# A graph network layer pair on one core: when each piece of the weights is asked for, and the queue that brings x

## The chip, the cores and the metric

The kernel runs on 1 core of one Trainium2 chip. The metric is the device time of one execution in microseconds. Six things work side by side in a core: TensorE (PE for its matmuls, PEld for the loading of its stationary operand), VectorE (DVE), ScalarE (ACT), GpSimd (POOL), SyncE (SP, here only an issuer of transfers) and 16 DMA engines.

## The reference

There are 96 nodes with 1024 features, 1632 edges, float32 throughout.

```python
h = relu(layernorm(x))
q, k, v = h @ wq.T + bq, h @ wk.T + bk, h @ wv.T + bv
q2, k2, v2 = q @ wiq.T + biq, k @ wik.T + bik, v @ wiv.T + biv      # 16 heads of 64
mask = -inf [N, N]; mask[src, dst] = softplus(type_weights)[edge_type - 1]
attn = softmax(q2 @ k2.T / 8 + mask)
x = x + (attn @ v2) @ wo.T + bo

h = relu(layernorm(x))
u = h @ root + bias
for r in range(8):                     # mean of the neighbours over edges of type r
    u = u + mean_r(h[src]) @ weight[r]
z = concat([u, h]) @ w_gate + b_gate
x = x + tanh(u) * z + h * (1 - z)
```

That makes 18 matrices of 1024x1024 (seven of the first layer, root, eight relations, and w_gate as two), 4 MB each and each used once: some 75 MB are read from HBM for an activation of only 96 rows.

## The kernel before, in words

The 18 matrices are read in the order of `SEQUENCE` (wq, wk, wiq, wik, wv, wiv, wo, root, the half of w_gate for x, the eight relations, the half of w_gate for u). Each is cut into four pieces of 1 MB (`PIECES`), so there are 72 pieces, numbered n = 0 to 71. A piece is 128 partitions x 2048 float32: half of the input features (four chunks of 128) by half of the output columns.

The pieces go through a ring of six slots of 1 MB in SBUF (`raw`, `SLOTS`). SyncE does nothing but ask for them. Its `fetch(n)` waits until piece n - 6 has been used (`piece_used`), because that piece sat in the same slot, and then issues the piece's transfers. The first four pieces go as one transfer of 1 MB each, all others as two of 512 KB (`transfers(n)`), the first with the even partitions, the second with the odd ones, one directly behind the other. `landed(n)` is the semaphore value of the slot that says that all of piece n is there.

TensorE walks through the same 72 pieces in the same order, in `piece` (L779), and in `gate_piece` (L1026) for the last four. A piece is 64 matmuls of a 128x64 block of weights against 96 columns, each with its own load of weights: four column chunks (`c`), four input chunks (`k`), two groups of 64 columns (`g`). The first waits for `landed(n)`; the last raises `piece_used`. Between pieces TensorE does the small work: transposes, the comparing of edges (L809, L820), the scores (L838), attn times v2 (L855), and the sums over neighbours (`sum_messages`, L967, behind the second piece of matrix WG_X, which is between pieces 33 and 34). DVE, ACT and POOL prepare and take what these need.

At the start x comes in two halves of 192 KB, columns 0 to 511 by SyncE's queue (ahead of the weights) and columns 512 to 1023 by ScalarE's queue (ahead of the biases, the edge lists and the type weights). DVE takes the statistics of each half (`bn_stats`, L504), and TensorE transposes x (L790). Then come the centring (L508), the transposing (L871), the copy into `uT` by ACT (L408) and the first piece.

Of the kernel before, what the change touches and what calls it, by code (L numbers as in the profile page):

```python
# [30 lines left out]
SLOTS = 6  # L31
# [5 lines left out]
def kind_of(n):  # L37
    return (KINDS_WIV if SEQUENCE[n // PIECES] == WIV else KINDS)[n % PIECES]


def transfers(n):

    return 1 if n < 4 else 2


def landed(n):

    return 16 * sum(transfers(i) for i in range(n % SLOTS, n + 1, SLOTS))
# [9 lines left out]
def gnn_kernel(nc, x, weights, biases, edge_columns, edge_rows, type_weights, out):  # L58
# [3 lines left out]
    CH = C // 2  # L62
# [17 lines left out]
    with ExitStack() as ctx:  # L80
        def sb(name, shape, dt=F32):
            return ctx.enter_context(nc.sbuf_tensor(name, shape, dt))

        def sem(name):
            return ctx.enter_context(nc.semaphore(name))

        raw = sb("raw", [P, SLOTS, CH * HALF])
        x_sb = sb("x_sb", [N, D])
# [74 lines left out]
        x_landed = [sem(f"x_landed{b}") for b in range(2)]  # L163
# [4 lines left out]
        raw_landed = [sem(f"raw_landed{s}") for s in range(SLOTS)]  # L168
        out_landed = sem("out_landed")
        piece_used = sem("piece_used")  # L170
        consts_ready = sem("consts_ready")
        vec = sem("vec")
        pool = sem("pool")
# [87 lines left out]
        def first_piece(m):  # L261
            return PIECES * SEQUENCE.index(m)
# [8 lines left out]
        def bank(t, b):  # L271
            return t[:, b, 0:TW]

        def half(t, b):
            return t[:, b * TW:(b + 1) * TW]

        def cols(t, b):
            return t[:, b * HALF:(b + 1) * HALF]
# [17 lines left out]
        @block.sync  # L296
        def _(sp):
            def fetch(n):
                where = PIECES * SEQUENCE[n // PIECES] + kind_of(n)
                if n >= SLOTS:  # L300
                    sp.wait_ge(piece_used, n - SLOTS + 1)
                for j in range(transfers(n)):
                    part = slice(j, P, transfers(n))
                    sp.dma_start(raw[part, n % SLOTS, :], weights[where, part]).then_inc(raw_landed[n % SLOTS], 16)

            sp.dma_start(cols(x_sb, 0), cols(x, 0)).then_inc(x_landed[0], 16)
            for n in range(N_PIECES):
                fetch(n)
            sp.wait_ge(out_first, 2)
            sp.dma_start(cols(out, 0), cols(out_rows, 0)).then_inc(out_landed, 16)  # L310
            sp.wait_ge(out_last, 1)
            sp.dma_start(out[:, D - P:D], out_rows[:, D - P:D]).then_inc(out_landed, 16)
            sp.wait_ge(out_landed, 48)
# [80 lines left out]

        @block.scalar
        def _(act):
            act.dma_start(cols(x_sb, 1), cols(x, 1)).then_inc(x_landed[1], 16)
            act.dma_start(bias_rows[:, :], biases.rearrange("m (c p) -> (m c) p", p=P)).then_inc(bias_landed, 16)
            act.dma_start(row_i, edge_rows).then_inc(rows_landed, 16)
            act.dma_start(edge_i[:, :], edge_columns).then_inc(edges_landed, 16)  # L400
# [368 lines left out]
        def _(pe):  # L769
            def piece(n, moving, a, opens=True, closes=True):  # L770

                s, kind = n % SLOTS, kind_of(n)
                b, k0 = kind // 2, CH * (kind % 2)
                pe.wait_ge(raw_landed[s], landed(n))
                for c in range(CH):
                    for k in range(CH):
                        for g in range(2):
                            at = k * HALF + c * P + g * HD
                            mm = pe.matmul(a[g * HD:(g + 1) * HD, b, c * N:(c + 1) * N], raw[:, s, at:at + HD],  # L779
                                           moving(k0 + k), start=opens and k0 == 0 and c == 0 and k == 0,  # L780
                                           stop=closes and k0 > 0 and c == CH - 1 and k == CH - 1)
                mm.then_inc(piece_used, 1)

            def of(t):
# [90 lines left out]
            n = first_piece(WQ)  # L875
            pe.wait_ge(h_ready, 2)
            piece(n, of(rT), acc[0])
            show_keys(0)
            show_keys(1)
            pe.wait_ge(diag_ready, 1)  # L880
            pe.wait_ge(h_ready, 4)
            pe.matmul(acc[1][:, 0, 0:N], ones_f[:, :], scale_diag[:, :], start=True, stop=True).then_inc(scale_shown, 1)
            piece(n + 1, of(rT), acc[0])
            piece(n + 2, of(rT), acc[0])
            piece(n + 3, of(rT), acc[0])

            n = first_piece(WK)
# [7 lines left out]
            n = first_piece(WIQ)  # L895
# [7 lines left out]
            n = first_piece(WIK)  # L903
# [7 lines left out]
            n = first_piece(WV)  # L911
# [8 lines left out]
            n = first_piece(WIV)  # L920
# [10 lines left out]
            n = first_piece(WO)  # L931
# [41 lines left out]
            n = first_piece(ROOT)  # L973
# [9 lines left out]
            for b in range(2):  # L983
                mm = pe.matmul(bank(side, b), ones[0:N, :], half(counts, b), start=True, stop=True)
# [8 lines left out]
            n = first_piece(WG_X)  # L993
# [9 lines left out]
            for r in range(R):  # L1003
                n = first_piece(REL0 + r)
# [29 lines left out]
            n = first_piece(WG_U)  # L1034
# [55 lines left out]
```

## Time and profile before

| | us |
|---|---|
| median of 3 runs | 228.63 (226.9 to 232.76) |
| the profiled execution, own time | 230.86 |
| its span, first to last instruction | 228.7 |
| PE busy | 217.3 (95%) |
| PEld busy | 210.8 (92%) |
| DVE / ACT / POOL busy | 80.5 / 22.3 / 24.6 |

The profiled execution is one execution; its own time is 2.16 us longer than its span. Busy time of PE is the union of its matmuls as recorded. PE and PEld work side by side. The part of the page with 40 slices shows the TensorE clock at nine tenths or more of full speed in each of them.

### The profile page before, as it was taken

What the parts mean: (1) busy time and instruction counts of PE and PEld (TensorE: products, weight loads), DVE (VectorE), ACT (ScalarE), POOL (GpSimd) and SP (SyncE); (2) the same over time, 40 slices, a digit from 0 to 9 for tenths busy, and PEclk for the clock granted to TensorE, in tenths of its full rate; (3) what the DMA queues carried; (4) which work ended last, traced back from release to release, by engine and by line L of the source; (5) the groups of instructions that cost most, each with busy time, mean ns of one, the idle gap of its engine ahead of it and who ended that gap; (6) DMA issues with size and microseconds to landing.
All of it is one profiled execution on the core that took longest, in us unless ns stands there. A gap on an engine that the chain in (4) does not pass through costs nothing.

```text
span 228.7 us, 10049 instructions
## 1 busy us (share of the span) xinstructions
PE 217.3 (95%) x4797; PEld 210.8 (92%) x4797; DVE 80.5 (35%) x138; ACT 22.3 (10%) x41; POOL 24.6 (11%) x53
## 2 busy tenths in 40 slices
PE   1999998999999999999999999999999999999894
PEld 1889998999999999799989999999999888999893
DVE  2459838051499731457466500000000000000614
ACT  2523000000020120313051000000000000000001
POOL 2255005400000000010003910000000000000000
PEclk9999999999999999999999999999999999999999
DMA  6999999999989989948981999999999999999202
GB/s 224 381 392 419 426 420 408 398 398 387 393 307 380 388 312 322 386 146 308 335 341 37 391 401 390 384 387 393 393 403 374 388 378 376 386 397 337 110 3 69
DMA packets 12363, 76.99 MB, mean 337 GB/s; under 512 B 2554, under 2 KB 2818, under 8 KB 3108
## 3 DMA queue, kind: packets, MB, share of 16 engines
q1 hardware_dynamic: 11792, 75.95, 85.9%
q8 instruction: 37, 0.61, 1.0%
q10 hardware_dynamic: 532, 0.42, 0.6%
q14 instruction: 2, 0.02, 0.0%
HBM read 75.97 MB, written 0.39 MB: 334 GB/s over the span
## 4 chain that ended last, share of the span: by engine, by line
PE 94%; DMA 2%; issue 1%; DVE 1%; ACT 0%
PE acc L779 81%; PE acc L1026 4%; DMA x_sb<-in_x 2%; PE turn L967 1%; PE side L827 1%; PE side L967 1%; PE side L1026 1%; PE turn L855 1%; DVE stats L504 1%; PE acc L797 1%; PE turn L797 0%; PE turn L871 0%; PE side L838 0%; PE turn L838 0%; PE acc L871 0%
## 5 line engine op out<-in xcount | busy, mean ns | idle before, releaser
L779 PE MATMUL acc<-mean,raw 128*64 128x96 f32 x2048 | 85.5, 246 | 1.4 <-issue 1.4
L779 PEld LDWEIGHTS acc<-mean,raw 128*64 128x64 f32 x2048 | 84.9, 137 | 1.8 <-issue 1.8
L779 PE MATMUL acc<-hT,raw 128*64 128x96 f32 x1024 | 44.7, 247 | 0.2
L779 PEld LDWEIGHTS acc<-hT,raw 128*64 128x64 f32 x1024 | 42.9, 137 | 1.5 <-issue 1.2
L742 DVE TENSOR_TENSOR uT<-acc,uT 128x384 f32<-128x384 f32 x2 | 1.1, 558 | 83.0 <-PE acc L779 83.0
L779 PE MATMUL acc<-qT,raw 128*64 128x96 f32 x512 | 22.0, 246 | 1.0 <-issue 1.0
L779 PEld LDWEIGHTS acc<-qT,raw 128*64 128x64 f32 x512 | 21.4, 137 | 1.3 <-issue 1.3
L779 PE MATMUL acc<-kT,raw 128*64 128x96 f32 x512 | 21.7, 246 | 0.0
L779 PEld LDWEIGHTS acc<-kT,raw 128*64 128x64 f32 x512 | 21.3, 137 | 0.3 <-issue 0.3
L779 PE MATMUL acc<-uT,raw 128*64 128x96 f32 x256 | 13.0, 271 | 0.0
L779 PEld LDWEIGHTS acc<-uT,raw 128*64 128x64 f32 x256 | 12.6, 156 | 0.3 <-ACT uT L408 0.2
L392 POOL TENSOR_TENSOR mean<-mean,per_count 128x384 f32<-128x384 f32 x8 | 8.4, 1079 | 23.5 <-DVE per_count L700 23.5
L465 ACT ACTIVATE gateT<-uT 128x384 f32<-128x384 f32 x2 | 1.0, 524 | 91.7 <-DVE uT L742 91.7
L1026 PE MATMUL acc<-uT,raw 128*64 128x96 f32 x192 | 8.7, 247 | 0.7 <-issue 0.7
L1026 PEld LDWEIGHTS acc<-uT,raw 128*64 128x64 f32 x192 | 8.3, 137 | 0.9 <-issue 0.9
L337 POOL TENSOR_TENSOR moments<-moments,pow_args 96x1 f32<-96x1 f32 x2 | 1.3, 636 | 56.6 <-DVE moments L683 56.5
L645 DVE STREAM_TRANSPOSE attnT<-attn 32x512 f32<-32x512 f32 x9 | 6.3, 701 | 0.3
L426 ACT ACTIVATE attn<-attn 96x768 f32<-96x768 f32 x2 | 1.7, 845 | 46.4 <-DVE attn L618 46.4
L790 PE MATMUL side<-ident,x_sb 96*128 96x96 f32 x8 | 1.5, 371 | 4.6 <-DMA x_sb<-in_x 4.6
L790 PEld LDWEIGHTS side<-ident,x_sb 96*128 96x128 f32 x8 | 1.2, 223 | 4.6 <-issue 4.6
L700 DVE RECIPROCAL per_count<-per_count 128x192 f32<-128x192 f32 x4 | 5.3, 1335 | 0.0
L580 DVE TENSOR_SCALAR mean<-node_iota,edge_tmp 102x384 f16<-102x384 f16 x16 | 5.3, 400 | 0.0
(177 smaller groups left out, 149.7 us busy)
## 6 DMA issues: line engine op xcount, KB each, us to landing
raw<-in_weights SPq DMA_DIRECT2D x136, 512.0 KB, 5.6
raw<-in_weights SPq DMA_DIRECT2D x4, 1024.0 KB, 9.8
x_sb<-in_x SPq DMA_DIRECT2D x1, 192.0 KB, 3.7
x_sb<-in_x ACTq DMA_DIRECT2D x1, 192.0 KB, 3.8
out<-out_rows SPq DMA_DIRECT2D x1, 192.0 KB, 2.1
out<-out_rows ACTq DMA_DIRECT2D x1, 144.0 KB, 2.2
out<-out_rows SPq DMA_DIRECT2D x1, 48.0 KB, 2.5
bias_rows<-in_biases ACTq DMA_DIRECT2D x1, 36.0 KB
```

The lines of the kernel that those rows point to most:

```text
L392: gp.tensor_tensor(mean[:, c, TW:2 * TW], mean[:, c, TW:2 * TW], half(per_count, 1), ALU.mult).then_inc(mean_later, 1)
L504: dve.bn_stats(stats[:, b, :], cols(x_sb, b)).then_inc(vec, 1)
L580: dve.tensor_scalar(rel_hot[:, c, :], node_iota[:, :], rel_key_f[:, c:c + 1], rel_step_f[:, c:c + 1], ALU.is_equal, ALU.mult).then_inc(rel ...
L645: dve.transpose(squares(attnT, j, i), squares(attn, i, j)).then_inc(attn_turned, 1)
L700: dve.reciprocal(span, span).then_inc(per_count_ready, 1)
L779: mm = pe.matmul(a[g * HD:(g + 1) * HD, b, c * N:(c + 1) * N], raw[:, s, at:at + HD], moving(k0 + k), start=opens and k0 == 0 and c == 0 a ...
L790: t = pe.transpose(dst[:, b, c * N:(c + 1) * N], src[:, (b * CH + c) * P:(b * CH + c + 1) * P], ident[0:N, 0:N])
L797: t = pe.transpose(dst[0:N, b, c * P:(c + 1) * P], src[:, (b * CH + c) * N:(b * CH + c + 1) * N], ident[:, :])
L827: pe.matmul(side[0:N, 0, 0:TW], src_hot[:, c, :], rel_hot[:, c, :], start=c == 0, stop=c == EC - 1).then_inc(counted, 1)
L855: mm = pe.matmul(turn[odd * HD:(odd + 1) * HD, h, j * N:(j + 1) * N], v2[0:N, head * HD:(head + 1) * HD], attnT[:, at:at + N], start=True, ...
L967: mm = pe.matmul(bank((turn, side)[c % 2], b), msgs[s][:, c * P:(c + 1) * P], half(counts, b), start=s == 0, stop=s == 1)
L1026: mm = pe.matmul(z[g * HD:(g + 1) * HD, :], raw[:, s, at:at + HD], of(uT)(k0 + k), start=k0 == 0 and k == 0 and (c == 0 or alone), stop=k0 ...
```

## The change

Three edits.

- **When a piece is asked for.** `lead(n)` is new: 4 for pieces 0 to 31, 5 for 32 to 38, 6 from 39 on. The first transfer of piece n now waits for piece n - lead(n) to be used. Four pieces go out without a wait, where six did.
- **Half a piece for half a piece.** The second transfer no longer follows directly. It waits until half of piece n + 1 - lead(n) has been used. For this `piece` raises a new semaphore, `step_used`, at the last matmul of its second column chunk.
- **x.** Both halves of x go out from SyncE's queue, one behind the other, ahead of the weights. ScalarE's queue now begins with the biases.

```diff
+STEPS = 2
+
 def transfers(n):
-
-    return 1 if n < 4 else 2
+    return 1 if n < lead(n) else STEPS
+
+
+def lead(n):
+    return 4 if n < 32 else 5 if n < 39 else SLOTS
...
             def fetch(n):
                 where = PIECES * SEQUENCE[n // PIECES] + kind_of(n)
-                if n >= SLOTS:
-                    sp.wait_ge(piece_used, n - SLOTS + 1)
                 for j in range(transfers(n)):
+                    if n >= lead(n) and j == 0:
+                        sp.wait_ge(piece_used, n + 1 - lead(n))
+                    if n >= lead(n) and j > 0:
+                        sp.wait_ge(step_used, (STEPS - 1) * (n + 1 - lead(n)) + j)
                     part = slice(j, P, transfers(n))
                     sp.dma_start(raw[part, n % SLOTS, :], weights[where, part]).then_inc(raw_landed[n % SLOTS], 16)
 
-            sp.dma_start(cols(x_sb, 0), cols(x, 0)).then_inc(x_landed[0], 16)
+            for b in range(2):
+                sp.dma_start(cols(x_sb, b), cols(x, b)).then_inc(x_landed[b], 16)
...
         def _(act):
-            act.dma_start(cols(x_sb, 1), cols(x, 1)).then_inc(x_landed[1], 16)
             act.dma_start(bias_rows[:, :], biases.rearrange("m (c p) -> (m c) p", p=P)).then_inc(bias_landed, 16)
...
+                    if c < CH - 1 and (c + 1) * STEPS % CH == 0:
+                        mm.then_inc(step_used, 1)
                 mm.then_inc(piece_used, 1)
```

## Rows read from the trace of the kernel before

**Rows 1.** The page, parts 1 and 2: engines, and the span in 40 slices.
```profile
PE 217.3 (95%) x4797; PEld 210.8 (92%) x4797; DVE 80.5 (35%) x138; ACT 22.3 (10%) x41; POOL 24.6 (11%) x53
DMA  6999999999989989948981999999999999999202
```

**Rows 2.** Waits of PE: who waited for what, us in total, times, longest.
```profile
PE side L790 <- DMA x_sb<-in_x: 4.6, 1, 4.6
PE acc L779 <- issue: 2.3, 4, 1.0
```

**Rows 3.** Waits of SyncE's queue, the same columns.
```profile
SPq L304 <- PE acc L779: 124.5, 66, 7.7
```

**Rows 4.** VectorE's timeline, two takes behind neighbouring pairs of pieces: start, duration.
```profile
53.76 0.56 DVE L489 TENSOR_TENSOR k2T<-acc,bias_cols 128x384 f32<-128x384 f32 x1 [5.04 <-PE acc L779]
56.40 0.56 DVE L489 TENSOR_TENSOR k2T<-acc,bias_cols 128x384 f32<-128x384 f32 x1 [2.08 <-PE acc L779]
```

**Rows 5.** The chain that ended last: start, us, what; all its pauses over 0.04 us after 8 us.
```profile
30.25 0.13 issue
...
36.21 0.96 issue
...
58.45 0.05 issue
...
180.19 0.51 issue
180.70 5.50 PE acc L779 x128
186.20 0.42 issue
186.62 5.50 PE acc L779 x128
192.12 0.42 issue
...
213.97 0.72 issue
```

**Rows 6.** The page, part 3: the queue of instructions; packets, MB, share of 16 engines.
```profile
q8 instruction: 37, 0.61, 1.0%
```

**Rows 7.** Transfers in 34.6 to 34.8, 178.4 to 178.6 and 128.0 to 128.2 us.
```profile
q8 instruction: 1, 0.02, 33.2%
...
q8 instruction: 1, 0.02, 30.0%
...
q8 instruction: 1, 0.02, 29.1%
```

**Rows 8.** Weight transfers (L304) asked for in 16-34, 34-56, 56-100, 150-172, 172-192 us.
```profile
DMA to landing us min/median/max: 6.8/7.9/9.1
...
DMA to landing us min/median/max: 4.6/5.5/8.0
...
DMA to landing us min/median/max: 3.8/4.8/6.6
...
DMA to landing us min/median/max: 4.9/5.6/6.9
...
DMA to landing us min/median/max: 4.6/6.2/8.3
```

**Rows 9.** Weight transfers asked for in 1.2-1.3 (piece 0) and 123.5-123.6 us (half of piece 40).
```profile
DMA to landing us min/median/max: 6.3/6.3/6.3
...
DMA to landing us min/median/max: 3.7/3.7/3.7
```

**Rows 10.** Windows: stretch, length, engines' busy time; last columns: granted clock, DMA share, GB/s.
```profile
38.00:56.00 18.00, 18.00 (x442) 18.00 (x440) 5.02 (x15) 0.00 (x0) 4.56 (x9) 1.00 1.01 398
178.00:196.00 18.00, 16.65 (x393) 16.20 (x391) 0.00 (x0) 0.00 (x0) 0.00 (x0) 1.00 0.99 381
```

**Rows 11.** Timeline of 0 to 16 us, the way to the first piece: start, duration, instruction.
```profile
0.81 0.39 SPq L306 DMA_DIRECT2D x_sb<-in_x  x1
0.81 0.42 ACTq L397 DMA_DIRECT2D x_sb<-in_x  x1
...
4.50 1.28 DVE L504 BATCH_NORM_STATS2 stats<-x_sb 96x6 f32<-96x512 f32 x2 [4.50 <-DMA x_sb<-in_x]
4.61 1.51 PE L790 MATMUL side<-ident,x_sb 96*128 96x96 f32 x8 [4.61 <-DMA x_sb<-in_x]
...
7.93 4.87 PE L779 MATMUL acc<-uT,raw 128*64 128x96 f32 x64
```

More of the change, by code:

```diff
@@ L170, in gnn_kernel @@
         piece_used = sem("piece_used")
+        step_used = sem("step_used")
         consts_ready = sem("consts_ready")
```

## The prediction

> **What bounds the kernel now.** I read the page first. TensorE is busy for 95% of the span, and so are the DMA engines in most slices [rows 1]. Two resources near their limit are a warning: busy shares alone don't say which one the other waits for. The waits do. In PE's list the only wait for a transfer is the one for x at the very start, 4.6 us; no piece of weights is ever waited for [rows 2]. SyncE's queue, in turn, waits 66 times for PE to free a slot, 124.5 us in all [rows 3]. So the transfers run ahead and the matmuls set the pace.
>
> That pace is read from VectorE's takes behind two neighbouring pieces of wik: 56.40 - 53.76 = 2.64 us for a piece of 64 matmuls [rows 4]. Against it 1 MB (1.049 million bytes) in 2.64 us is 397 GB/s, and the DMA engines move 398 at a share of 1.01 where PE runs without a break [rows 10]. There is next to no spare rate. 72 pieces at 2.64 us are 190 of the 228.7 us. The rest is PE's small work, the start, and pauses.
>
> The pauses are the third thing to read, from the chain that ended last [rows 5]. Seven times PE stands still in the middle of a run of matmuls with nothing to wait for that the profile knows ("issue"). Two things give away what they are. The last three before 196 us lie exactly 128 matmuls apart, which with their 128 loads are 256 instructions. And the page has a queue of instructions with 37 packets and 0.61 MB [rows 6], some 16 KB each, while PE and PEld ran 2 x 4797 = 9594 instructions [rows 1], which is 37.5 times 256. So PE's program itself arrives over the DMA engines, 256 instructions at a time, among the weights. Such a packet begins in 178.4 to 178.6 and PE goes on at 180.70; one begins in 34.6 to 34.8 and PE goes on at 36.21 + 0.96 = 37.17 [rows 5, 7]. A block is thus usable 2.1 to 2.6 us after its packet begins. Stepping back from the pause at 180.19 in blocks of 2 x 2.64 = 5.28 us gives 132.67 for an earlier block's first need; its packet began at 128.0 to 128.2 [rows 7], usable by 130.4, with 2.2 us to spare, and there was no pause. The pauses are packets of instructions that came late.
>
> What a pause costs is more than its idle time, since the last matmul's recorded end covers some. From 180.70 to 186.62 are 5.92 us for a block that takes 5.28: 0.64 lost where the chain shows 0.42, so 0.22 is to be added to each. The first three: 0.13 + 0.96 + 0.05 + 3 x 0.22 = 1.80 us. The last four: 0.51 + 0.42 + 0.42 + 0.72 + 4 x 0.22 = 2.95 us. Together 4.75 us.
>
> Why late? The time from asking for weights to their landing says how much data stands in line. A half piece with nothing before it takes 3.7 us [rows 9]. By stretch the median is 7.9 us in 16-34, 5.5 in 34-56, 4.8 in 56-100, 5.6 in 150-172 and 6.2 in 172-192 [rows 8]. Four of the seven pauses follow the two stretches with a line of 6 us and more. The pause at 58 us costs little and 214 us is near the end, so the tie isn't strict, but it is what speaks for the change.
>
> **The change part by part.**
>
> *Lead of four, halves asked for apart (pieces 4 to 31, to about 100 us).* The first half of piece n is asked for when three pieces are still to be used, so it has 3 x 2.64 = 7.92 us. The second half goes 1.32 us later and has 6.6 us. Transfers that are spaced like this need 3.7 us when nothing is in line, or 4.5 if a half follows a half at the rate of 1.32 us (3.7 + 1.32 - 0.52, the spacing of two issues being about 0.5). That leaves 2 us or more, so no wait of PE; the line before the engines drops from two or three halves to about one. The first three pauses go: -1.80 us. Bounds: they stay (0), or the margin breaks (second rival).
>
> *Lead of five, then six (pieces 32 to 71).* From piece 39 on the slots are as full as before. Only the second half is asked for 1.32 - 0.5 = 0.8 us later, which shortens its time in line but not the work. PE still takes weights as fast as the engines bring them, so a line can build up as in 172-192 us. But a request for instructions that comes in the first half of a piece then has one half less before it, worth up to 1.3 us, and the late blocks missed by 0.64 to 0.94 us. I take two thirds of the last four pauses as gone: -2.0 us, between 0 and -2.95. The first weights behind the neighbour sums (pieces 38 to 40) are asked for later than before, since the second half of 38 waits for half of piece 34. The cover is the depth: they have over 7 us against 6.
>
> *x.* The chain to the first piece begins with x: asked for at 0.81, used at 4.50 [rows 11]. The second half now goes about 0.44 us later, on the queue of the first. It is needed only when the first statistics are done, at 4.50 + 0.64 = 5.14, and would land at about 4.9 where it landed at 4.6: nothing. Piece 0 is asked for at about 1.7 where it was 1.25; it landed 6.3 us after that, at 7.55, and PE began it at 7.93 [rows 9, 11], so 0.38 us of the 0.45 are covered, and as the bytes ahead of it are the same on either queue I take 0. Bounds: -0.2 (x alone on its way is quicker) to +0.5. ScalarE's biases and edge lists go out 0.4 us sooner, off the chain. The first piece takes 4.87 us in place of 2.64; nothing in the change touches that.
>
> *step_used.* One more signal from a matmul that runs anyway, 68 times, and one more wait of SyncE for each piece. SyncE has nothing else in its queue, and behind the waiting transfer stand only later pieces. The same kind of signal and wait stands at every piece already, and the pace of 2.64 us is 64 even steps across it. 0; at most, if each cost what one matmul's step does (2.64 / 64 = 0.04 us), 68 x 0.04 = 2.7 us.
>
> Sum on the profiled execution: 230.86 - 1.80 - 2.0 + 0 = 227.1. The runs shown spread from 226.9 to 232.76, and without any pause the profiled one would be at 230.86 - 4.75 = 226.1, just under the lowest. I read the spread as pauses that fall differently in each run. The median run, at 228.63, then has less to give than the profiled one, and both should come out near the same place, about 1 us above 226.1. I forecast 227.0.
>
> A rule that speaks on this: the Trainium skill (DMA: Bandwidth & Descriptors, Queues, rings and completion order) says that each DMA engine takes turns between its queues packet by packet. A packet of instructions would then wait for one packet of weights, not for the line, and the lead would not matter (first rival). Another (Runtime: NRT & Kernel Launch, Instruction fetch mechanics) says that the instructions come in 16 KiB blocks fetched ahead, at a cost "mostly hidden". The sizes agree with the 0.61 MB in 37 packets; seven pauses of PE say that it isn't hidden here.
>
> **The rivals.**
>
> *The line doesn't matter.* The instruction packet is late for another reason, such as a slow round of its own request, and takes turns with the weights. For it: the pause at 58 us stands where the line was near 5.5 us, and most blocks between 122 and 172 us were in time at 5.6. Then pauses stay as they are, and the median with them: 228.6. Its milder form: the line matters, but from piece 39 on it is as long as before; then 1.8 us go in the profiled run, and of the median's 2.5 us above 226.1 about 0.9: 227.7.
>
> *The margin breaks (slower).* PE begins to wait for weights with a lead of four. For it: the engines are at a share of 1.01 where PE runs unbroken, and landing times of up to 8.3 us occur [rows 8, 10]. It decides where the second half lands more than 6.6 us after it is asked for. The loss is then shared by three pieces: with 8.3 us for half of the 28 pieces it is 14 x 1.7 / 3 = 7.9 us, and 227.0 + 7.9 = 235. Against it: those times include the wait of the second half behind its own first half and a line made by the lead of six, and in 56-100 us, the better part of this stretch, the longest was 6.6.
>
> *Everything goes and the start gains.* 226.1 - 0.2, and by the spread of the runs down to 224.
>
> **How the numbers follow.** Forecast 227.0 with a chance of 0.42 (its own range 225.9 to 228.2). Milder form, 227.7: 0.18. Unchanged, 228.6: 0.18, with the spread of a median 227.3 to 230. Margin breaks, 229 to 237: 0.12, two thirds of it over 233.2. Everything goes, 224 to 226: 0.10, some over 2%. A measurement of this kernel tells about 2% (4.6 us) from no change. Faster by more than that needs more than all pauses of the median run: 0.06; slower 0.08; within 0.86. For 8 in 10 the range runs from 225.2 to 230.3.
>
> **What would show it.** Right: no "issue" pause before 100 us, at most one or two small ones after 170; landing times near 4 to 5 us in 16-56 us; PE's only wait for a transfer is still x; the first piece still starts near 7.9. Wrong: PE waits on `raw` at L779 with a DMA as releaser between 16 and 100 us; pauses of "issue" 256 instructions apart with landing times under 5 us, which would mean that the line is not the cause; a pace other than 2.64 us for a piece, which would put a price on the signal; a first piece later than 8.4. The forecast itself fails if the spread of the runs comes from something other than these pauses.

## The result and the profile after

The changed kernel takes 238.09 us (median of 4 runs, 236.67 to 240.01) against 229.57 us for the kernel before (226.9 to 232.76). The ratio is 1.0459, with a 95% interval of 1.0316 to 1.0601. It is slower by 4.6%, where the forecast was 227.0 us. Ratios here and below leave out runs over 1.5% above the fastest of their kernel, so they can differ from the quotient of the medians, which are over all runs. Line numbers shift: L779 of before is L792, L304 is L317.

The profiled execution took 240.01 us, its span is 237.8 us. Its waits of PE (who waited for what, us in total, times, longest):

```profile
PE acc L792 <- issue: 4.9, 8, 1.1
PE acc L792 <- DMA raw<-in_weights: 4.5, 2, 3.6
PE side L805 <- DMA x_sb<-in_x: 3.9, 1, 3.9
```

[rows 2] had no wait for weights. Now there are two, 3.6 us before the first piece and 0.9 us before piece 21. The chain that ended last says where (start, us, what):

```profile
1.74 9.19 DMA raw<-in_weights
...
11.06 5.39 PE acc L792 x64
...
61.84 1.08 issue
...
72.06 7.44 DMA raw<-in_weights
...
144.12 0.28 issue
...
161.20 0.42 issue
...
172.40 0.51 issue
...
183.63 0.49 issue
...
194.91 0.52 issue
...
206.20 0.52 issue
...
217.50 1.07 issue
```

The first row is the start: piece 0, asked for at 1.74, is there 9.19 us later, and PE begins it at 11.06 where it began at 7.93 [rows 11]. The second transfer in the chain is the second half of piece 21, which PE waits for until 79.54, in the middle of the stretch with the short lead. Between the first piece and 125 us the chain has five pauses of "issue", 1.44 us in all; from 125 us on it has nine, 4.11 us. In the kernel before these were three, 1.14 us, and four, 2.07 us [rows 5].

The start in the timeline (start, us, instruction):

```profile
0.81 0.88 SPq L320 DMA_DIRECT2D x_sb<-in_x  x2
3.78 1.49 DVE L517 BATCH_NORM_STATS2 stats<-x_sb 96x6 f32<-96x512 f32 x2 [3.78 <-DMA x_sb<-in_x]
...
7.21 0.65 ACT L421 ACTIVATE uT<-acc 128x192 f32<-128x192 f32 x2
11.06 5.39 PE L792 MATMUL acc<-uT,raw 128*64 128x96 f32 x64 [3.57 <-DMA raw<-in_weights]
```

x itself is sooner, 3.78 against 4.50 us [rows 11], and what PE needs of it is ready by 7.9. The weights are late. The transfers in four stretches of this kernel (stretch, length, busy times, clock, DMA share, GB/s):

```profile
4.00:8.00 4.00, 3.17 (x17) 2.49 (x17) 3.70 (x10) 1.66 (x6) 1.24 (x4) 1.00 0.85 268
...
12.00:18.00 6.00, 6.00 (x66) 5.18 (x64) 0.81 (x2) 3.27 (x6) 1.33 (x7) 1.00 0.68 269
18.00:24.00 6.00, 6.00 (x150) 6.00 (x150) 5.97 (x8) 0.00 (x0) 1.66 (x1) 1.00 0.73 225
40.00:56.00 16.00, 15.81 (x378) 15.46 (x375) 6.08 (x18) 0.00 (x0) 5.99 (x12) 1.00 0.95 368
```

and the first three and the last in the kernel before:

```profile
4.00:8.00 4.00, 3.17 (x19) 2.73 (x21) 3.36 (x10) 1.33 (x5) 1.24 (x4) 1.00 0.99 389
...
12.00:18.00 6.00, 6.00 (x122) 5.38 (x120) 4.15 (x8) 2.33 (x6) 4.13 (x14) 1.00 0.97 389
18.00:24.00 6.00, 6.00 (x152) 6.00 (x150) 5.97 (x5) 0.94 (x1) 2.31 (x1) 1.00 1.02 425
40.00:56.00 16.00, 16.00 (x394) 16.00 (x392) 3.99 (x11) 0.00 (x0) 2.73 (x7) 1.00 1.00 398
```

Two things are to be read here. Only four pieces are asked for until the first is used up at 16.45 us, so the engines are partly idle (share 0.68 in 12 to 18 us). And what they move for each unit of busy time is less: 225 / 0.73 = 308 GB/s in 18 to 24 us against 425 / 1.02 = 417. That is not the short lead by itself: e16 and e17 below, with the same lead but without the spacing and with x as before, have 348 / 0.97 = 359 and 392 / 1.01 = 388 in that stretch.

```profile
18.00:24.00 6.00, 6.00 (x150) 6.00 (x148) 5.97 (x5) 0.40 (x1) 2.44 (x1) 1.00 1.01 392
```

The weight transfers asked for in 16-34, 150-172 and 172-192 us took, from asking to landing (L317):

```profile
DMA to landing us min/median/max: 3.6/5.6/6.5
...
DMA to landing us min/median/max: 5.2/5.9/7.2
...
DMA to landing us min/median/max: 5.5/5.8/6.9
```

Early on that is shorter than [rows 8] (7.9), as intended. Later it is about the same, 5.9 against 5.6 in 150 to 172 us and 5.8 against 6.2 in 172 to 192 us, though every second transfer is now asked for 0.8 us later.

The 9.15 us between the two profiled executions (240.01 - 230.86): first piece begun later 11.06 - 7.93 = 3.1; first piece itself 5.39 - 4.87 = 0.5; the wait for weights after that 4.5 - 3.6 = 0.9 idle and about 0.2 covered, as the prediction worked it out for pauses, 1.1; pauses of instructions before 125 us 1.44 + 5 x 0.22 = 2.5 against 1.8; behind 125 us 4.11 + 9 x 0.22 = 6.1 against 2.95. The sum is 8.6; some 0.6 us are left over.

The same account fits every profile below. From its span take the "issue" pauses behind the first piece (with 0.22 us for each), PE's waits for weights behind the first piece, and what the first piece begins later than 7.93 us. The spans go from 222.7 to 237.8 us; what is left goes only from 222.9 to 225.6 us in all 20 profiles. So late blocks of instructions, late weights and a late start are where the kernels differ.

### The profile page after: what moved, and what is told of

Read it like the earlier page. It is cut to its first block, busy times and chain, and to the rows that moved or that the text cites. A ratio compares the mean times of both kernels' runs of the same rounds, so it can differ in the third digit from the quotient of the medians.

```text
span 237.8 us, 10049 instructions
## 1 busy us (share of the span) xinstructions
PE 220.2 (93%) x4797; PEld 211.5 (89%) x4797; DVE 80.6 (34%) x138; ACT 22.3 (9%) x41; POOL 22.8 (10%) x53
## 4 chain that ended last, share of the span: by engine, by line
PE 88%; DMA 7%; issue 2%; SPq 0%; ACT 0%
PE acc L792 76%; DMA raw<-in_weights 7%; PE acc L1041 3%; PE turn L982 1%; PE side L842 1%; PE side L982 1%; PE side L1041 1%; PE turn L870 1%; PE acc L812 1%; PE turn L812 0%; PE side L853 0%; SPq L320 0%; PE turn L824 0%; PE turn L853 0%; PE side L835 0%
## 5 line engine op out<-in xcount | busy, mean ns | idle before, releaser
L792 PE MATMUL acc<-mean,raw 128*64 128x96 f32 x2048 | 86.7, 246 | 4.1 <-issue 3.8
L792 PEld LDWEIGHTS acc<-mean,raw 128*64 128x64 f32 x2048 | 85.1, 137 | 5.6 <-issue 5.6
L792 PE MATMUL acc<-hT,raw 128*64 128x96 f32 x1024 | 45.0, 247 | 1.2 <-issue 1.1
L792 PEld LDWEIGHTS acc<-hT,raw 128*64 128x64 f32 x1024 | 42.9, 137 | 2.9 <-issue 2.4
L792 PE MATMUL acc<-qT,raw 128*64 128x96 f32 x512 | 22.0, 247 | 0.9 <-DMA raw<-in_weights 0.9
L792 PE MATMUL acc<-kT,raw 128*64 128x96 f32 x512 | 22.4, 247 | 0.3
L792 PEld LDWEIGHTS acc<-qT,raw 128*64 128x64 f32 x512 | 21.3, 137 | 1.3 <-DMA raw<-in_weights 1.1
L792 PEld LDWEIGHTS acc<-kT,raw 128*64 128x64 f32 x512 | 21.5, 137 | 1.0 <-issue 1.0
L792 PE MATMUL acc<-uT,raw 128*64 128x96 f32 x256 | 13.5, 277 | 3.6 <-DMA raw<-in_weights 3.6
L792 PEld LDWEIGHTS acc<-uT,raw 128*64 128x64 f32 x256 | 13.1, 160 | 3.9 <-issue 3.8
L1041 PEld LDWEIGHTS acc<-uT,raw 128*64 128x64 f32 x192 | 8.3, 137 | 0.0
L502 DVE TENSOR_TENSOR kT<-acc,bias_cols 128x384 f32<-128x384 f32 x4 | 2.2, 558 | 8.0 <-PE acc L792 8.0
```

Source lines behind the costliest of these rows:

```text
L502: dve.tensor_tensor(by_chunk(half(dst, b)), by_chunk(bank(a, b)), bias_of(bias, b), ALU.add).then_inc(taken, 1)
L1041: mm = pe.matmul(z[g * HD:(g + 1) * HD, :], raw[:, s, at:at + HD], of(uT)(k0 + k), start=k0 == 0 and k == 0 and (c == 0 or alone), stop=k0 ...
```

## The experiments

Each row of the table is one kernel. "Before" is the kernel before in the same set of runs. A time varies from run to run by several us (the kernel before from 227.35 to 235.64 over 69 runs in five sets), so small gaps rest on the whole series and not on one line. The pauses are those of one profiled execution each: idle time of the "issue" pauses over 0.04 us in the chain behind the first piece, before and from 125 us on.

| run | what | median (runs) | before | ratio, interval | issue before / from 125 us |
|---|---|---|---|---|---|
| e1 | x alone | 232.2 (8) | 231.72 | 1.0101, 1.004 to 1.016 | 0.46 / 0 |
| e2 | lead and halves, x as before | 236.72 (4) | 231.72 | 1.0315, 0.9996 to 1.063 | 2.57 / 3.40 |
| e3 | lead alone | 229.55 (10) | 231.72 | 0.9954, 0.988 to 1.003 | 1.46 / 1.74 |
| e4 | halves alone, lead 6 | 233.5 (4) | 231.72 | 1.0237, 1.015 to 1.033 | 1.08 / 2.21 |
| e5 | e1, small transfers held | 233.97 (2) | 229.35 | - | 0.16 / 2.26 |
| e6 | second half of x last in ScalarE's queue | 238.76 (2) | 229.35 | 1.0429, 1.026 to 1.060 | 1.91 / 0 |
| e7 | e2 in quarters | 233.28 (4) | 229.35 | 1.0189, 1.009 to 1.029 | 0.05 / 0.20 |
| e8 | e2 in whole pieces | 231.35 (4) | 229.35 | - | 0 / 3.14 |
| e9 | halves at three quarters, lead 6 | 231.69 (11) | 230.15 | 1.0109, 1.006 to 1.016 | 3.82 / 1.56 |
| e10 | e4 again | 234.37 (5) | 230.15 | 1.0229, 1.014 to 1.032 | 3.01 / 4.41 |
| e11 | kernel before again | 228.0 (11) | 230.15 | 0.9939, 0.989 to 0.999 | 2.38 / 0 |
| e12 | x in ScalarE's queue | 231.95 (4) | 230.15 | 1.0106, 1.001 to 1.020 | 0.73 / 0 |
| e13 | before + 64 instructions | 234.15 (4) | 231.5 | 1.0193, 1.007 to 1.032 | 0.50 / 0.54 |
| e14 | e2, halves up to piece 38 | 236.08 (4) | 231.5 | 1.0193, 0.996 to 1.042 | 1.81 / 4.70 |
| e15 | e2, halves from piece 39 | 232.97 (4) | 231.5 | 1.0131, 1.002 to 1.025 | 1.58 / 2.61 |
| e16 | e3 again | 227.33 (4) | 231.5 | 0.9889, 0.971 to 1.007 | 0 / 0.34 |
| e17 | e3, five rounds | 227.67 (6) | 230.54 | 0.9895, 0.981 to 0.998 | 0 / 0 |
| e18 | lead 4 for all pieces | 228.36 (10) | 230.54 | 0.9883, 0.982 to 0.995 | 1.60 / 1.17 |

### The parts one by one (e1 to e4)

e1, x alone:

```diff
-            sp.dma_start(cols(x_sb, 0), cols(x, 0)).then_inc(x_landed[0], 16)
+            for b in range(2):
+                sp.dma_start(cols(x_sb, b), cols(x, b)).then_inc(x_landed[b], 16)
-            act.dma_start(cols(x_sb, 1), cols(x, 1)).then_inc(x_landed[1], 16)
```

> The kernel before with one edit: both halves of x from SyncE's queue. Theory A (the short lead lets the DMA engines run dry): x costs nothing, ratio 1.00, first piece begins near 7.9 us. Rival X (the start is lost because x stands ahead of the weights and ScalarE's small transfers now run beside the first weights): first piece begins near 11 us as in the changed kernel, ratio 1.013 to 1.017.

Rival X. PE's waits in e1:

```profile
PE side L790 <- DMA x_sb<-in_x: 4.1, 2, 3.8
PE acc L779 <- DMA raw<-in_weights: 2.3, 1, 2.3
```

The first transfer took 8.3 us to land, and the first piece began at 10.19. The engines moved 231 GB/s in 4 to 8 us at a share of 0.83; before it was 389 at 0.99.

```profile
4.00:8.00 4.00, 3.28 (x17) 2.44 (x16) 3.29 (x10) 1.25 (x5) 1.24 (x4) 1.00 0.83 231
```

This is no chance of one profile. In the 15 profiles of kernels that bring x as the kernel before does, the first transfer lands in 5.9 to 6.3 us and the engines move 384 to 405 GB/s in that stretch; with both halves of x ahead of it on its queue it lands in 9.2 (the changed kernel), 8.3 (e1) and 7.3 us (e5). The start loses 2.3 us. The medians differ by 0.5 only, the ratio is 1.0101; late instructions vary by more than 2.3 us from run to run, and e1's profile, the fastest of its eight runs, had almost none.

e2, the changed kernel with x as before:

```diff
-            for b in range(2):
-                sp.dma_start(cols(x_sb, b), cols(x, b)).then_inc(x_landed[b], 16)
+            sp.dma_start(cols(x_sb, 0), cols(x, 0)).then_inc(x_landed[0], 16)
...
+            act.dma_start(cols(x_sb, 1), cols(x, 1)).then_inc(x_landed[1], 16)
```

> The changed kernel with x put back on two queues; lead and spacing as changed. Theory A: the first piece is late by about 3 us all the same, because only four pieces are in line, and the ratio is that of the changed kernel, 1.035 to 1.045. Rival X: first piece near 7.9 us, ratio 1.02 to 1.03.

Theory A's claim on the start is refuted: the first piece begins at 7.7 with four pieces in line. The medians put lead and halves together at +5.0 us; the interval of the ratio just includes 1.

e3, the lead without the spacing (against e2):

```diff
                     if n >= lead(n) and j == 0:
                         sp.wait_ge(piece_used, n + 1 - lead(n))
-                    if n >= lead(n) and j > 0:
-                        sp.wait_ge(step_used, (STEPS - 1) * (n + 1 - lead(n)) + j)
```

> The kernel before with the lead of 4, 5 and 6 pieces, but the second half asked for right behind the first. Theory A: PE waits for weights and the transfers are slow before 100 us; from 130 us on as before, since the lead is 6 there; ratio 1.01 to 1.02. Rival H (asking in halves is the cost): ratio 1.00, no waits for weights.

Neither weights nor time were lost: 229.55 against 231.72 us, and PE's list has no wait for weights. Theory A falls. What costs is the spacing, or the spacing in company with the lead.

e4, the spacing alone (against e2):

```diff
-    return 1 if n < lead(n) else STEPS
+    return 1 if n < 4 else STEPS
...
-    return 4 if n < 32 else 5 if n < 39 else SLOTS
+    return SLOTS
```

> The kernel before with lead 6 throughout, but the second half of each piece asked for half a piece later. Theory A: no waits for weights anywhere, ratio 1.00 to 1.005. Rival H (the spacing makes the packets of instructions late): pauses of issue about 11 us apart from 140 us on, and before 100 us too, some 0.7 us each, ratio 1.015 to 1.03.

Rival H in the time (233.5), and no waits for weights. The pauses of this profile (the fastest of the four runs) are hardly more than those of the kernel before, 3.29 against 3.21 us of idle time, so by itself it doesn't show where the time goes. e10 repeats the kernel with 234.37 against 230.15, and its profile, a run of 237.31 us, has sixteen pauses, 7.42 us, and no wait for weights. Over both sets the mean of 9 runs is 3.3 us above that of the 38 runs of before.

### The start (e5, e6, e12)

e5, against e1:

```diff
+            act.wait_ge(x_landed[1], 16)
             act.dma_start(bias_rows[:, :], biases.rearrange("m (c p) -> (m c) p", p=P)).then_inc(bias_landed, 16)
```

> As e1 (both halves of x on SyncE's queue), but ScalarE's four small transfers (biases, edges, type weights) wait until x has landed. Reading: when the last share of piece 0 lands, which was 7.5 us before and 10.1 in e1. Theory X1 (the small transfers, which now start 0.4 us sooner and run beside the first weights, hold the engines up): piece 0 lands near 7.5 again, though the biases come late. Rival X2 (it is x itself, ahead in the queue of the weights): piece 0 lands near 10 still.

The first transfer took 7.3 us from 1.7, so piece 0 landed at 9.0: between the two, 1.0 us of e1's lateness gone. The first piece began only at 13.35, for another reason (PE waited 6.6 us for the biases).

e6, against the kernel before:

```diff
-            act.dma_start(cols(x_sb, 1), cols(x, 1)).then_inc(x_landed[1], 16)
...
             act.dma_start(tw_in[:, :], type_weights.to_broadcast([N, 4])).then_inc(types_landed, 16)
+            act.dma_start(cols(x_sb, 1), cols(x, 1)).then_inc(x_landed[1], 16)
```

> The kernel before, but the second half of x is the last in ScalarE's queue, behind the four small transfers. Theory X1: the small transfers go out as early as in e1, and piece 0 lands near 10 us though x is on two queues. Rival X2: piece 0 lands near 7.5 us. In both the second half of x itself lands later, near 6 us.

Piece 0 landed 5.2 us after it was asked for, the fastest of all, with the small transfers as early as in e1. That speaks against X1 as the main cause, though holding the small transfers in e5 gave back 1.0 us. But the expectation for x itself was far off: 14.1 us to land, not some 4. PE's list of e6:

```profile
PE side L790 <- DMA x_sb<-in_x: 15.8, 2, 12.0
PE acc L779 <- issue: 1.8, 2, 1.2
```

Why a transfer of 192 KB takes so long beside pieces of weights, these runs do not show.

e12, against the kernel before:

```diff
-            sp.dma_start(cols(x_sb, 0), cols(x, 0)).then_inc(x_landed[0], 16)
...
-            act.dma_start(cols(x_sb, 1), cols(x, 1)).then_inc(x_landed[1], 16)
+            for b in range(2):
+                act.dma_start(cols(x_sb, b), cols(x, b)).then_inc(x_landed[b], 16)
```

> The kernel before with both halves of x in ScalarE's queue, none in SyncE's. Theory X2 (x in the weights' own queue, ahead of them, delays the first weights): piece 0 lands by 7.5 us or earlier, since it is asked for 0.4 us sooner, and the time is that of before within 1%. Rival (x and weights disturb each other whatever the queue): piece 0 lands near 9 to 10 us.

Piece 0 took 6.2 us from 0.8 and was there by 7.0, as X2 says. But the two halves of x took 6.6 us (median), PE then waited 1.2 us for the biases behind them, and the first piece began at 12.73, 4.8 us later than in the kernel before. The time is 1.1% above that of before, with an interval that reaches down to 0.1%. The issues of x in e6 and in e12 (queue, size, us to landing):

```profile
x_sb<-in_x SPq DMA_DIRECT2D x1, 192.0 KB, 2.8
x_sb<-in_x ACTq DMA_DIRECT2D x1, 192.0 KB, 14.1
```
```profile
x_sb<-in_x ACTq DMA_DIRECT2D x2, 192.0 KB, 6.6
```

So in these arrangements the second half of x delayed either the weights (ahead of them on their own queue) or itself (on ScalarE's queue behind another transfer). One half on each queue, each first, as the kernel before has it, was the best of the five arrangements tried. Why the weights start slowly behind x on one queue was not found.

### The size and the moment of the parts (e7 to e11, e13)

e7 and e8, against e2:

```diff
-STEPS = 2
+STEPS = 4      # e7; in e8: STEPS = 1
```

> As e2 (lead 4, 5, 6; x on two queues), but each piece in four transfers of 256 KB, asked for a quarter of a piece apart. Theory R (engines that have run empty start each new transfer slowly, and asking in small spaced parts makes them run empty more often): more waits for weights and more late instructions than e2, 240 us or more. Rival P (only the moment at which the second half is asked for matters, against the moment of the request for instructions): within 1% of e2, 235 to 238 us.

> As e2, but each piece in one transfer of 1 MB, asked for when piece n - lead has been used. Theory R: fewest restarts, so no later than the lead alone (e3, 229.6 us): 228 to 231 us, and few late instructions. Rival P: the same, since nothing is asked for in the middle of a piece; so only a time over 233 us would speak against both.

e7 took 233.28 us, 3.9 us above the kernel before in its set, where e2 was 5.0 us above it in its own. Theory R, 240 us or more, is refuted; that quarters are better than halves is not shown. Its kind of loss is another one altogether:

```profile
PE acc L792 <- DMA raw<-in_weights: 4.0, 7, 1.0
PE acc L1041 <- DMA raw<-in_weights: 0.9, 1, 0.9
```

Eight waits for weights, 4.9 us, and next to no late instructions (0.25 us in the chain). e8 is the reverse: no wait for weights, and five late blocks, two of them over 1 us:

```profile
183.15 1.06 issue
...
206.65 1.25 issue
```

In these two profiles small transfers go with late weights and punctual instructions, and large ones the other way round; with halves and the same lead (e2) both occur. Each is one profile, and late instructions alone vary from 0 to 3.2 us of idle time between profiles of one program (e3, e16, e17), so that the size is the reason is suggested, not shown. In the medians neither gained on the kernel before (229.35).

e9, against e4 (the signal behind the third column chunk and not the second):

```diff
-                    if c < CH - 1 and (c + 1) * STEPS % CH == 0:
+                    if c == 2:
                         mm.then_inc(step_used, 1)
```

> As e4 (lead 6 throughout), but the second half is asked for when three quarters of a piece are used, not half. Theory P (what counts is how much is in line at the moment when TensorE's next block of instructions is asked for, which from 125 us on is about 0.3 us behind the middle of a piece): the second half now comes after that moment, instruction packets begin 1 to 3 us after their request where e4 has 2.2 to 4.6, and the time falls back to that of before or under it: 228 to 231 us. Rival R (spacing itself makes the engines run empty and slow): as e4 or worse, 233 us and more.

231.69 us: nearer to theory P than to R by the time. But its chain has nine pauses, 5.38 us, so it isn't right by P's mechanism. Its median is 1.5 us above that of the kernel before. e11 below, which is the kernel before once more, lies 2.15 us under it in the same set, so that a cost of asking at three quarters of a piece is likely, but not shown.

e10 and e11, against e4 and the kernel before:

```diff
+            for _ in range(96):
+                pe.nop()
             pe.wait_ge(consts_ready, 1)
```

They were to move TensorE's blocks of instructions against the pieces. The traces show that they moved nothing: up to the same pause PE has as many matmuls in e10 as in e4 (x603), and the pauses of e11 and of the kernel before also stand behind 603. The stretches up to that pause, e4 first (length, busy times with the number of instructions):

```profile
0.00:36.80 36.80, 31.67 (x603) 30.07 (x604) 21.12 (x34) 7.94 (x14) 9.72 (x32) 1.00 0.96 381
0.00:36.20 36.20, 31.20 (x603) 29.69 (x604) 21.30 (x35) 7.94 (x14) 9.88 (x33) 1.00 0.94 379
```

So e10 is e4 again and e11 the kernel before again, and nothing of their expectations was tested.

> As e4, with 96 empty instructions for TensorE in its idle time before x lands, which moves the blocks of 256 instructions against the pieces by three quarters of a piece. Theory P: blocks are then asked for just before a piece ends, about 1 us after the last half was asked for; fewer late blocks than e4, 229 to 232 us. Rival R: no change against e4, 233 us.

> The kernel before with the same 96 empty instructions. Theory P: blocks are asked for just before the two halves of the next piece instead of 1.1 us behind them; the line then is at its shortest, so at most as many late blocks as before and 0.5 to 1.5% faster. Rival R: no change.

e11 is useful as a measure of chance: the same program as before gave 228.0 against 230.15 us beside it, ratio 0.9939 with an interval that just excludes 1. Differences under 1% in one set are not to be trusted.

e13, against the kernel before (`spare` is a new semaphore that nothing waits for):

```diff
+            for i in range(64):
+                pe.sem_inc(spare, 1)
             pe.wait_ge(consts_ready, 1)
```

> The kernel before with 64 real instructions more for TensorE (signals of an unused semaphore) in its idle time before x lands; they move the blocks of 256 instructions by half a piece, so from 125 us on a block is asked for about 0.5 us before the first half of a piece is, where before it is 0.8 us behind. Theory P (the moment against the line decides): packets begin later or sooner after their request than in the kernel before in all pieces from 125 us on, sooner if the line as a whole counts: 226 to 229 us. Rival S (the moment doesn't matter; the lateness comes in spells whatever the place): same as before within 1%, pauses now at another place in the pieces, in spells.

The signals took until 10.79 us and PE's first piece began at 13.63, 5.7 us later than in the kernel before. That is more than the whole loss of 2.65 us, so the rest of the kernel was faster than usual, and the pauses from 125 us on were 0.54 us. The pauses came near the end of a piece in place of its middle (the pause behind 603 matmuls stands behind 571 here), so the blocks were moved by 32 matmuls and their loads, which is 64 instructions. But e1, e6, e11 and e12 have no pause there at all with the blocks unmoved, so this decides nothing between P and S.

### Where the spacing costs (e14, e15), and the lead again (e16 to e18)

e14 and e15, against e2; e16 and e17 are e3 unchanged:

```diff
-                    if n >= lead(n) and j > 0:
+                    if lead(n) <= n < 39 and j > 0:      # e14; in e15: n >= 39 and j > 0
```

> As e2 (lead 4, 5, 6; x on two queues), but halves asked for apart only up to piece 38. If the cost of spacing is in the short lead: 233 to 235 us, with waits for weights near pieces 5, 13 and 22 and late blocks before 100 us, and after 130 us as in e3. If it is in the later part: 230 us.

> As e2, but halves asked for apart only from piece 39 on. If the cost is in the later part: 233 us or more, with late blocks of 4 to 6 us in all after 130 us and none of the waits for weights before 100. If it is in the short lead: 230 us.

> e3 once more, the lead of 4, 5 and 6 alone, beside e14 and e15. It should be within 1% of the kernel before, 228 to 231 us, and below e14 and e15 by what the spacing costs in each part; if it is 233 or more, the gap between e3 and e2 was chance.

236.08, 232.97 and 227.33 us, beside 231.5 for the kernel before. Against e16, which differs from each by the spacing alone, spacing costs in both parts; that it costs more in the early one is so in the medians, with four runs of each. The surprise is e14's late part, whose conditions for asking are those of e16, and whose chain there had ten pauses:

```profile
139.50 0.53 issue
145.52 0.42 issue
151.44 0.42 issue
...
203.28 0.42 issue
```

e16 had one of 0.34 us. But e3, the same program as e16, had five there (1.74 us against e14's 4.70), so chance has a large part in this. The landing times point the same way as the pauses: weights asked for in 125 to 150 us took 7.0 us (median) in e14 against 5.2 in e16 and 4.9 in e3. It looks as if what happens before piece 39 is carried on. In e14 the second half of piece 38 waits for half of piece 34, which comes behind the neighbour sums, so the ring is filled half a piece later. The engines work at the rate at which TensorE uses the weights (398 against 397 GB/s), so a lateness once given isn't made up. That is an inference from [rows 10] and from e14, not shown; no run measured the refilling by itself.

> The lead of 4, 5 and 6 alone (as e3 and e16), now in five rounds. If the step of the forecast on the lead was right (fewer late blocks before 100 us): 1 to 2% faster than the kernel before, 226 to 229.5 us. Rival: e16 was a lucky set and it is the same, 229.5 to 231.5 us.

227.67 against 230.54 us, ratio 0.9895 with the interval 0.981 to 0.998. Its chain has no pause and its PE list one line:

```profile
PE side L803 <- DMA x_sb<-in_x: 4.4, 1, 4.4
```

Weight transfers asked for in 16 to 34 us in e17:

```profile
DMA to landing us min/median/max: 4.5/5.0/5.9
```

Over e3, e16 and e17 the mean of 20 runs is 2.3 us below that of 41 runs of before. In view of e11 I call the lead alone not slower, and probably 1% faster. It is the version to keep.

e18, against e17:

```diff
-    return 4 if n < 32 else 5 if n < 39 else SLOTS
+    return 4
```

> As e17 with a lead of 4 for all pieces. Theory L (fewer pieces in line, fewer late blocks): as e17 or up to 1% below it. Rival M (with 4 pieces the transfers don't keep pace with TensorE where it runs for 20 pieces without a break): waits for weights from piece 45 on, 232 us or more.

228.36 us, 0.9883: no wait for weights with a lead of four throughout, so rival M falls; nor is it better than the lead of 4, 5 and 6, so no gain from a smaller lead in the later part is seen.

## Why the prediction was wrong, point by point

For the profiled execution the prediction gave 227.1 us; it took 240.01. Of these 12.9 us the late start with the slower first piece is 3.6 (forecast 0), the wait for weights 1.1 (forecast 0), the late instructions before 125 us 2.5 (forecast 0), and those from 125 us on 6.1 - 0.95 = 5.1.

- **What bounds the kernel, and what the pauses are.** Right for the pace and the pauses. TensorE's pace, read from VectorE's takes as in [rows 4], is 2.64 us for a piece in the changed kernel (59.81 - 57.17) and in e4 (56.35 - 53.71) too, so the signal of `step_used` costs nothing visible. In all 20 profiles the pauses over 0.3 us stand behind the same numbers of matmuls, 127 or 128 apart or a multiple of that (476, 603, 3794, 3922, 4050 and so on); in e13, where the instructions were moved, they stand 32 matmuls earlier.
- **Lead of four, "-1.80 us".** Failed in the changed kernel, whose first part lost 2.5 us to late instructions where the kernel before lost 1.8. The lead by itself has the right sign in the times (e3, e16, e17, e18). Its profiles are divided: e16 and e17 have no pause before 125 us, e3 has one of 1.46 us and e18 four, 1.60 us, so "the first three pauses go" isn't a rule even for it.
- **"That leaves 2 us or more, so no wait of PE".** Failed, for the spaced halves. I took 3.7 to 4.5 us for a transfer in a short line, from one transfer that began on idle engines. Measured are 5.6 us (median) in 16 to 34 us, against 6.6 to spare, and 7.4 at the longest in 56 to 100 us. The rival took 8.3 us for the longest landing time; [rows 8] has 9.1. e2, e7, e14 and e15 all have waits for weights in PE's list, that of e15 (0.7 us) at 47 us, where it asks with the lead alone; e3, e16, e17 and e18 have none. So the spacing made them common, and the margin was thin without it. The second rival named this and priced it at 8 us; behind the first piece it was 1.1 us in the profile.
- **"Only the second half is asked for 0.8 us later, which shortens its time in line": -2.0 us.** Failed, and in sign. The time in line did not shorten as a whole (5.9 against 5.6 us in 150 to 172 us, 5.8 against 6.2 in 172 to 192 us). From 125 us on 6.1 us were lost in place of 2.95 (forecast 0.95). This is the largest error. That the spacing costs time is shown by e2 against e3 and by e14 and e15 against e16, each pair in one set, and by e4 and e10; the profiles of e2, e10 and e14 have 3.40, 4.41 and 4.70 us of idle time in this part, that of e4 only 2.21. By which way it delays the instructions is open. That work asked for later is done later where there is no spare rate can't be the whole of it, since the shorter lead also asks later and cost nothing.
- **x, "I take 0", bounds -0.2 to +0.5.** Failed: +2.3 us alone (e1), 3.1 in the profile of the change. The estimate counted bytes ahead in the queue and took for granted that the engines work at the same rate from the first moment. They did not (231 and 268 GB/s in 4 to 8 us against 389). Why stays open.
- **The median would have less to give than the profiled run, all near 226.1.** Partly right: with the lead alone, runs with next to no pauses are there (e17, 224.86 us, and e16, 226.94), the first of them lower than the 226.1 that I worked out. In e17 the first piece took 3.79 us against 4.87, which I had taken as fixed; it took 3.72 (e9) to 5.39 us (the changed kernel) in the profiles. Why is open.
- **The first rival (the line doesn't matter).** Not refuted, but the landing times of all profiles speak against it. The prediction's own tie rested on [rows 8], where five and not four of the seven pauses lie in the two stretches with the long line or within 2.3 us behind them. Take the 18 profiles with two transfers of 512 KB for a piece, and the median landing time of the weights asked for in 125 to 212 us. It is 5.0 to 5.3 us in the five with no late block there, 5.3 to 5.7 in the nine with 0.3 to 2.6 us of pauses, and 5.8 to 6.0 in the four with over 3 us. One of the first group and one of the last, e17 and the changed kernel:

```profile
DMA to landing us min/median/max: 4.5/5.2/6.5
...
DMA to landing us min/median/max: 3.7/5.8/7.2
```

  Weights and instructions are late together; which makes which late, or what makes both, these rows don't say. e7 and e8 suggest that the size of a transfer matters as well. The Trainium skill (DMA: Bandwidth & Descriptors, Queues, rings and completion order) has engines take turns between queues by packets; no run here measured a turn; e6, where a transfer of 192 KB took 14.1 us beside the pieces of weights, would fit turns that are long. It does not explain that e11, the same program as the kernel before, has none where that one has four late blocks. What sets off a spell of late blocks stays open.

## What to carry to other kernels

In this kernel the DMA engines have to run at nearly their full rate to feed TensorE. There a lead of four pieces in place of six cost nothing, but asking for the second half of each piece later by itself cost 2% (e4, e10): a smoother line on paper has to be tried before it is believed. A wait for a resource that is busy nearly all the time should be priced with the landing times under load of the same stretch, not with those of a transfer on idle engines. And the two halves of x, on which the start depends, were best each first on a queue of its own; putting both ahead of the weights cost 2.3 us of the start, and putting the second behind the small transfers 11.5 us (7.93 to 19.46).

## What was not expected of the hardware

- TensorE's instructions come 256 at a time over the same DMA engines. When such a packet is late, TensorE stops: 4.75 us of the profiled run before, about 8.6 us after (5.55 idle in 14 pauses, and 0.22 for each), none in e17.
- With the size of the weight transfers the kind of wait changed, in one profile of each. At 256 KB: 0.25 us of late instructions, 4.9 us of waits for weights. At 1 MB: 3.14 us and none.
- Two transfers of 192 KB put ahead of it on its queue made the first 1 MB transfer land in 7.3 to 9.2 us (three profiles), against 5.9 to 6.3 us with one (15 profiles).
- A 192 KB transfer took 2.8 us at the head of SyncE's queue, and 14.1 us when it was fifth in ScalarE's queue beside 1 MB pieces on SyncE's.
- 64 signals of a semaphore at the head of TensorE's program took until 10.79 us, where its first matmul had been at 4.61: about 0.1 us for each, or 0.17 if they had the whole time from the start.
- Two groups of runs of the same program in one set differed by 0.9% in their medians (228.0 and 230.15 us).
